# A mixture-of-experts stage rebuilt from four masked experts for every token to lists of one expert each

## What is computed

```python
x = hidden_states.reshape(-1, H)                     # 4096 tokens, H = 128, already normalised
expert_idx = jnp.argmax(x @ W_router, axis=-1)       # one of E = 4
h = jnp.einsum('th,ehi->tei', x, W1) + b1            # I = 512
h = jax.nn.gelu(h, approximate=False)
onehot = jax.nn.one_hot(expert_idx, E, dtype=x.dtype)
intermediate = jnp.einsum('te,tei->ti', onehot, h)
y = intermediate @ Wo + bo + x                       # Wo is one matrix for all experts
y = _layer_norm(y, ln_gamma, ln_beta)                # eps 1e-12
...
x = x + _layernorm(_L0_ffn_ref(_layernorm(x, axis=-1), ...), axis=-1)
```

## Time and profile before

| | us |
|---|---|
| median of 3 runs | 560.15 (558.89 to 562.59) |
| the profiled execution | 559.23 |
| its span, first to last instruction | 557.4 |
| TensorE busy | 506.9 |
| VectorE busy | 424.0 |
| GpSimd busy | 338.8 |
| ScalarE busy | 298.3 |

### The profile page before, as it was taken

One profiled execution on the slowest core, in us unless ns is written; L12 is line 12 of the kernel. 1 busy time (PEld: TensorE's weight loads), 2 busy tenths in 40 slices (PEclk: granted clock), 3 DMA queues, 4 the chain that ended last, 5 costly groups with the idle time before them and its releaser, 6 DMA issues. The chain is left out here.

```text
span 557.4 us, 16662 instructions
## 1 busy us (share of the span) xinstructions
PE 506.9 (91%) x5277; PEld 312.7 (56%) x5280; DVE 424.0 (76%) x1954; ACT 298.3 (54%) x820; POOL 338.8 (61%) x799
## 2 busy tenths in 40 slices
PE   8878679999999999999999998869999999999991
PEld 3434324556556665555555665535677677577671
DVE  5986696988888888998899887645647777675655
ACT  2665305888888888888888888713212211211110
POOL 4799202688888888688888889960122343333241
PEclk9999855999999999999999999989999999999997
DMA  4466450332112332123331100000000000000001
GB/s 128 137 214 176 150 98 2 101 92 69 49 27 59 81 63 64 38 41 63 62 64 40 27 4 4 4 1 1 0 1 1 20 19 0 19 20 0 20 19 38
DMA packets 49058, 28.09 MB, mean 50 GB/s; under 512 B 6808, under 2 KB 48056, under 8 KB 48976
## 3 DMA queue, kind: packets, MB, share of 16 engines
q1 hardware_dynamic: 47648, 26.73, 19.0%
q10 hardware_dynamic: 1328, 0.36, 0.3%
HBM read 17.90 MB, written 8.91 MB: 48 GB/s over the span
## 5 line engine op out<-in xcount | busy, mean ns | idle before, releaser
L1096 DVE CUSTOM_DVE_ANT_0 added<-psS,maskq 128x256 bf16<-128x256 f32 x512 | 200.5, 414 | 34.8 <-PE psS L937 21.9
L1316 ACT ACTIVATE probs<-psST 128x512 f32<-128x512 f32 x240 | 143.2, 597 | 43.2 <-PE psST L973 41.7
L973 PE MATMUL psST<-qst,kst 50*128 50x128 bf16 x992 | 101.0, 222 | 0.0
L937 PE MATMUL psS<-kst,qst 48*128 48x256 bf16 x448 | 91.5, 286 | 2.4 <-DVE rowmax L1096 1.3
L994 PE MATMUL psPV<-probs,vst 128*10 128x128 f32 x1984 | 79.9, 277 | 11.9 <-POOL probs L1231 8.1
L1760 ACT ACTIVATE hT<-fpsH 128x512 f32<-128x512 f32 x32 | 19.1, 597 | 121.7 <-PE fpsH L1504 121.7
L1228 POOL TENSOR_SCALAR_AFFINE_SELECT probs<-probs 128x256 f32<-128x256 f32 x150 | 61.7, 412 | 4.3 <-ACT probs L1316 4.1
L1231 POOL TENSOR_SCALAR_AFFINE_SELECT probs<-probs 128x256 f32<-128x256 f32 x150 | 61.2, 408 | 0.0
L937 PEld LDWEIGHTS psS<-kst,qst 48*128 48x128 bf16 x448 | 25.2, 95 | 62.6 <-issue 36.3
L994 PEld LDWEIGHTS psPV<-probs,vst 128*10 128x10 f32 x1984 | 43.9, 91 | 27.1 <-issue 16.6
L973 PEld LDWEIGHTS psST<-qst,kst 50*128 50x128 bf16 x992 | 55.8, 95 | 0.0
(11 more groups left out here) (198 smaller groups left out, 1092.5 us busy)
## 6 DMA issues: line engine op xcount, KB each, us to landing
q_parts<-early SPq DMA_DIRECT2D x8, 384.0 KB, 2.6
k_parts<-early SPq DMA_DIRECT2D x8, 384.0 KB, 2.7
qst<-q_parts SPq DMA_DIRECT2D x32, 96.0 KB
kst<-k_parts SPq DMA_DIRECT2D x32, 96.0 KB
X<-in_L_attn_x_dram SPq DMA_DIRECT2D x8, 256.0 KB, 3.3
qst<-q_parts SPq DMA_DIRECT2D x32, 64.0 KB
kst<-k_parts SPq DMA_DIRECT2D x32, 64.0 KB
out_dram<-res SPq DMA_DIRECT2D x8, 256.0 KB, 2.3
```

What stands on the lines that cost most here:

```text
L937: last = nc.tensor.matmul(bank[:, a], q, kst[rows, slot, ring(n - 1, 2)], start=True, stop=True)
L973: last = nc.tensor.matmul(bank[:, a, side * P:(side + 1) * P], kst[rows, slot, ring(n - 1 + side)], qst[rows, slot, ring(n)], start=not ma ...
L1096: taken = nc.vector.tensor_tensor_reduce(added[:, 2 * (g % 2) + a], psS[g % 2][:, a], mask, 1.0, NEG * 4, ALU.add, ALU.max, rowmax[:, n.mo ...
L1316: nc.scalar.activation(probs[:, g ^ 1], psST[g % 2][:].rearrange("p a c -> p (a c)"), ACT.Exp, scale=SCALE).then_inc(s_exp.sem, 1)
```

## The change

`attend` writes the residual to columns 128 to 255 of a new tile `rows` (257 floats for each token; column 256 holds the token's number, by an `iota` in `project`). In steps 3 to 21 of `attend`, ScalarE's queue issues one DMA a step that fills a block of 512 rows of the new DRAM tensor `by_expert` with blank rows (19 blocks of 526 KB). `project` gains 33 small `memset`s and one of 128 x 256 on VectorE. The bias is loaded by partition (`b1T`, four DMAs of 4-byte pieces), and nine VectorE operations that prepared the bias in three parts, and one on ScalarE, go; one small one (`tri`) comes.

`ffn` has two parts now:

1. Routing, chunk by chunk (8): turn, copy, logits, one-hot row with a sign (`choose`, 6 VectorE operations), the token's rank in its expert's list by small matmuls with a triangle of ones (`ranks`), its place (`places`, 5 VectorE operations), and on GpSimd four indirect DMAs of 128 rows of 1028 bytes to these places in `by_expert` (`move`). Experts 0 and 1 share a region and grow from its two ends, as do 2 and 3. Then `map_slots`, some 22 dependent VectorE operations on 11 to 44 columns, works out which expert and which block each of 11 slots has.
2. Slots (11, of 512 rows of one expert; 8 chunks and at most 3 partly filled blocks more): SyncE reads the numbers into a register, copies that expert's weights within SBUF (2 DMAs of 256 KB) and loads the block. TensorE turns it, and makes only the 12 matmuls of the one expert (before: 48 and 4 for the bias). The bias goes into ScalarE's GELU. Spread, mask and multiply are gone. Layer norms as before, split otherwise over the engines: VectorE the first and its statistics, ScalarE the second (`normed`). GpSimd writes the results by four indirect DMAs of 128 rows of 512 bytes, to the rows that column 256 names; blank rows lie out of bounds and are dropped.

```diff
+SLOT = CH
+NS = NCH + E - 1
+PAIR_ROWS = T + SLOT
+PAIR_SLOTS = PAIR_ROWS // SLOT
+SPARE = 2 * PAIR_SLOTS
+ROW = 2 * D + 1
...
+            nc.vector.memset(held.blank[:, 0:2 * D], 0.0)
+            nc.vector.memset(held.blank[:, 2 * D:ROW], 1.0)
...
+                    if g == 7 and 3 <= s.k < 3 + SPARE + 1:
+                        block = s.k - 3
+                        act.dma_start(by_expert[block * SLOT:(block + 1) * SLOT].rearrange("(t p) w -> p t w", p=P),
+                                      held.blank[:].unsqueeze(1).broadcast_to([P, CT, ROW])).then_inc(s_blank, 16)
...
+            def load_weights(i):
+                r = i % W_RING
+                e = sp.value_load(expert[0:1, i:i + 1], min_val=0, max_val=E - 1)
+                sp.wait_ge(s_h.sem, s_h.after(nth_slot(i - W_RING)))
+                for k, parts in enumerate((w1hi, w1lo)):
+                    sp.dma_start(w1[:, r, k].bitcast(F32),
+                                 parts[:, bass.ds(e, 1)].rearrange("k o i -> k (o i)").bitcast(F32)).then_inc(s_w1[r], 16)
+            def load_tile(i):
+                r = i % TILE_RING
+                a = sp.value_load(slot[0:1, i:i + 1], min_val=0, max_val=SPARE)
+                if i >= TILE_RING:
+                    n = i - TILE_RING
+                    sp.wait_ge(s_store[n % 2], 16 * CT * (n // 2 + 1))
+                sp.dma_start(tile[:, r], by_expert.rearrange("(n t p) w -> p n t w", p=P, t=CT)[:, bass.ds(a, 1)]
+                             .rearrange("p o t w -> p (o t) w")).then_inc(s_tile[r], 16)
+            sp.wait_ge(s_map, MAPPED)
+            for i in range(W_RING):
+                load_weights(i)
+            sp.wait_ge(s_moved, 16 * NB)
+            for i in range(W_RING):
+                load_tile(i)
+            for i in range(W_RING, NS):
+                load_tile(i)
+                load_weights(i)
...
+            def ranks(c):
+                pe.wait_ge(s_oh.sem, s_oh.after(c))
...
+                nc.tensor.matmul(psP[:, 0:CT * E], held.tri[:], flat, start=True, stop=False)
+                for t in range(1, CT):
+                    nc.tensor.matmul(psP[:, t * E:CT * E], filler[:, 0:P], flat[:, 0:(CT - t) * E], start=False,
+                                     stop=(t == CT - 1))
+                for t in range(CT):
+                    last = nc.tensor.matmul(psP[:, CT * E:(CT + 1) * E], filler[:, 0:P], signed[:, t],
+                                            start=(t == 0), stop=(t == CT - 1))
+                last.then_inc(s_rank.sem, 1)
+            turned(chunk(0))
+            logits(chunk(0))
+            for c in range(NCH):
+                keep_warm(nc, psY[1][:], filler, 4)
+                ranks(chunk(c))
+                if c + 1 < NCH:
+                    turned(chunk(c + 1))
+                    logits(chunk(c + 1))
+            keep_warm(nc, psY[1][:], filler, 24)
...
+            def hidden(n, j):
+                u, r = n.mod(2), n.k % W_RING
+                pe.wait_ge(s_gelu.sem, s_gelu.after(n, j + 1 - 2))
+                if j == 0:
+                    pe.wait_ge(s_w1[r], 32 * (n.k // W_RING + 1))
+                    pe.wait_ge(s_lo.sem, s_lo.after(n))
+                cols = slice(j * P, (j + 1) * P)
+                for k, (w, x) in enumerate(((0, xhi), (1, xhi), (0, xlo))):
+                    last = nc.tensor.matmul(psH[j % 2][:], w1[:, r, w, cols], x[:, u], start=(k == 0), stop=(k == 2))
+                last.then_inc(s_h.sem, 1)
...
+            for i in range(-1, NS + 1):
+                n = nth_slot(i)
+                if (n + 1).live:
+                    transposed(n + 1)
                 if n.live:
+                    hidden(n, 0)
+                    hidden(n, 1)
+                if (n - 1).live:
+                    outputs(n - 1)
                 if n.live:
+                    hidden(n, 2)
+                    hidden(n, 3)
...
+            def choose(c):
+                lg = psR[:, 0:CT * E].rearrange("p (t e) -> p t e", e=E)
+                dve.wait_ge(s_logit.sem, s_logit.after(c))
+                nc.vector.tensor_reduce(lmx[:], lg, AX.X, ALU.max).then_inc(s_oh.sem, 1)
+                dve.wait_ge(s_oh.sem, s_oh.after(c, 1))
+                nc.vector.tensor_tensor(iseq[:], lg, lmx[:].unsqueeze(2).broadcast_to([P, CT, E]),
+                                        ALU.is_equal).then_inc(s_oh.sem, 1)
+                dve.wait_ge(s_oh.sem, s_oh.after(c, 2))
+                nc.vector.tensor_tensor(rank[:], iseq[:], prio[:].unsqueeze(1).broadcast_to([P, CT, E]),
+                                        ALU.mult).then_inc(s_oh.sem, 1)
+                dve.wait_ge(s_oh.sem, s_oh.after(c, 3))
+                nc.vector.tensor_reduce(rmx[:], rank[:], AX.X, ALU.max).then_inc(s_oh.sem, 1)
+                dve.wait_ge(s_oh.sem, s_oh.after(c, 4))
+                nc.vector.tensor_tensor(onehot[:], rank[:], rmx[:].unsqueeze(2).broadcast_to([P, CT, E]),
+                                        ALU.is_equal).then_inc(s_oh.sem, 1)
+                dve.wait_ge(s_oh.sem, s_oh.after(c, 5))
+                nc.vector.tensor_tensor(signed[:], onehot[:], held.sign[:].unsqueeze(1).broadcast_to([P, CT, E]),
+                                        ALU.mult).then_inc(s_oh.sem, 1)
+            def places(c):
+                dve.wait_ge(s_rank.sem, s_rank.after(c))
+                nc.vector.tensor_tensor(place[:], psP[:, 0:CT * E].rearrange("p (t e) -> p t e", e=E),
+                                        following[:].unsqueeze(1).broadcast_to([P, CT, E]), ALU.add)\
+                  .then_inc(s_place.sem, 1)
+                dve.wait_ge(s_place.sem, s_place.after(c, 1))
+                nc.vector.tensor_tensor(following[:], following[:], psP[:, CT * E:(CT + 1) * E], ALU.add)\
+                  .then_inc(s_place.sem, 1)
+                nc.vector.tensor_tensor(own_place[:], place[:], onehot[:], ALU.mult).then_inc(s_place.sem, 1)
+                dve.wait_ge(s_place.sem, s_place.after(c, 3))
+                nc.vector.tensor_reduce(place_f[:], own_place[:], AX.X, ALU.add).then_inc(s_place.sem, 1)
+                dve.wait_ge(s_place.sem, s_place.after(c, 4))
+                nc.vector.tensor_copy(where[:, c.times(CT):c.times(CT, CT)], place_f[:]).then_inc(s_place.sem, 1)
+
...
+            norm.statistics(dve, chunk(2))
+            for i in range(NCH):
+                c = chunk(i)
+                choose(c)
+                if (c + 3).live:
+                    norm.statistics(dve, c + 3)
+                if (c + 2).live:
+                    norm.apply(dve, c + 2)
+                places(c)
...
+            def low(n):
+                dve.wait_ge(s_hi.sem, s_hi.after(n))
+                nc.vector.tensor_tensor(xlo[:, u], psT[u][:], xhi[:, u].bitcast(F32), ALU.subtract).then_inc(s_lo.sem, 1)
+            def scaled(n):
+                u = n.mod(2)
+                dve.wait_ge(s_rs2.sem, s_rs2.after(n))
                 for t in range(CT):
+                    last = nc.vector.scalar_tensor_tensor(out=y2[:, t], in0=y1[:, t], scalar=mv2[:, u, t, 0:1],
+                                                          in1=gamma[:], op0=ALU.subtract, op1=ALU.mult)
+                last.then_inc(s_y2.sem, 1)
+                dve.wait_ge(s_y2.sem, s_y2.after(n))
+                dve.wait_ge(s_y5.sem, s_y5.after(n - 2))
                 for t in range(CT):
+                    last = nc.vector.scalar_tensor_tensor(out=y4[:, u, t], in0=y2[:, t], scalar=rstd2[:, u, t:t + 1],
+                                                          in1=beta[:], op0=ALU.mult, op1=ALU.add)
+                last.then_inc(s_y4.sem, 1)
+                dve.wait_ge(s_y4.sem, s_y4.after(n))
+                dve.wait_ge(s_rs3.sem, s_rs3.after(n - 2))
+                statistics(s_st3, n, 1, lambda t: y4[:, u, t], mv3)
...
+            def result(n):
+                u = n.mod(2)
+                dve.wait_ge(s_y5.sem, s_y5.after(n))
+                if n.k >= 2:
+                    dve.wait_ge(s_store[u], 16 * CT * (n.k // 2))
+                nc.vector.tensor_tensor(res[:, u], y5[:, u], tile[:, n.k % TILE_RING, :, D:2 * D], ALU.add)\
+                  .then_inc(s_res.sem, 1)
+            def summed(n):
+                u = n.mod(2)
+                dve.wait_ge(s_Y.sem, s_Y.after(n))
+                dve.wait_ge(s_XF.sem, s_XF.after(n))
+                nc.vector.tensor_tensor(y1[:], psY[u][:].rearrange("p (t d) -> p t d", t=CT), XF[:, u], ALU.add)\
+                  .then_inc(s_y.sem, 1)
+                dve.wait_ge(s_y.sem, s_y.after(n))
+                dve.wait_ge(s_rs2.sem, s_rs2.after(n - 2))
+                statistics(s_st2, n, 0, lambda t: y1[:, t], mv2)
+            for i in range(-1, NS + 4):
+                n = nth_slot(i)
+                if (n + 1).live:
+                    low(n + 1)
+                if (n - 2).live:
+                    scaled(n - 2)
+                if (n - 3).live:
+                    result(n - 3)
+                if (n - 1).live:
```

(75 more changed lines are left out.)

588 lines of the change are left out of this document (236 added, 352 removed).

## The result

The changed kernel takes 608.7 us (median of 4 runs, 607.22 to 609.31), the kernel before 561.3 beside it on the same chip: a ratio of 1.085, with a 95% interval of 1.080 to 1.089. The prediction was 587 us with a range of 545 to 640; the result lies above the band of 570 to 605 that the prediction held likeliest. The profiled execution had 609.26 us and a span of 607.5.

The account below looks back on a forecast made before the run. The prediction took TensorE to bound `ffn` before, and a loop through GpSimd's stores and VectorE after. Stage start 380.9, routing 52.2, tile load 4.5, slots 147.2 and 1.8 around the span gave 587 us, range 545 to 640.

Parts of the forecast that it names:

- rival (b): In the slots VectorE locks GpSimd out while it makes addresses: C = 14.6, total 631 us; chance 0.11.
- start of the stage: Work added ahead of `ffn` shifts its start from 375.9 to 380.9 us; removed bias operations in `attend` taken as 0.
- s: Time one indirect DMA's issue takes in GpSimd's queue: taken as 1.1 us, between bounds of 0.45 and 2.16.
- R: Routing's length, by GpSimd's 32 indirect DMAs or the map: max(17 + 32s, 46) us, 52 at s = 1.1.
- S: All slots with filling and draining: 98.8 + 44s, 147 us at s = 1.1.
- C: One slot's turn through GpSimd, VectorE and the four stores on GpSimd: 7.4 + 4s, 11.8 us at s = 1.1.
- Fill and drain: Ends of the slots: `scaled(1)` starts at 24 us; after nine turns come 8.1 + 8s us.
- Price 0: TensorE's clock drops after pauses in the slots cost nothing: some 2 us of 7.2, still under C.
- (a): Indirect DMA issue is cheap, s = 0.45: total 552 us, faster by 1.3%; chance 0.17.
- (c): Each indirect DMA issue takes 2.16 us: R = 86, S = 194, total 667 us; chance 0.06.
- (e): The slots' loop is as priced but s lies at 0.6 to 0.75: 558 to 565 us, no difference; chance 0.12.
- (d): Blank writes stall `attend` by 2.16 us a step: total 624 us; chance 0.04.

Follow-up runs that it names:

- 3: Changed kernel with twelve filler matmuls on TensorE ahead of each slot's first hidden group: 614.15 us, ratio 1.099 to the kernel before.
- 8: Changed kernel with half of the routing's indirect DMAs left out (two of four tiles of each chunk not moved): 603.2 us, ratio 1.079 to the kernel before.
- 5: Changed kernel with the first norm's root ahead of the stores, `XF` replaced by one-row bias matmuls on TensorE, `low` after `scaled`: 597.73 us, ratio 1.068.
- 10: Changed kernel with the first norm's root ahead of the stores and eight filler matmuls a slot on TensorE: 588.71 us, ratio 1.052 to the kernel before.
- 1: Changed kernel with the first norm's root put ahead of the four indirect stores in GpSimd's order: 577.02 us, ratio 1.034 to the kernel before.

## Why the prediction came out as it did

The sign and the mechanism were right, and the time lies in the range, 22 us over the forecast. That the miss isn't larger is in part luck: three terms were together 31 us too low, and the start of the stage, put 8 us too late, hid a quarter of that. The upper end of the range came from rival (b), not from the terms that ran over. Of the signs that the prediction gave, the turn came out at 13.8 us and not 11 to 12, and TensorE's busy share in the slots at 69% (85.17 of 124 us) and not 60%. Term by term (us):

| term | forecast | measured |
|---|---|---|
| start of the stage | 380.9 | 372.9 |
| routing to the last landing | 52.2 | 56.8 |
| tile load to the first transposes | 4.5 | 4.7 |
| slots, first transposes to the end | 147.2 | 173.2 |
| around the span | 1.8 | 1.8 |

**The bound of the kernel before.** Right. With TensorE's work gone, nothing on it sets the turns of the changed kernel (3).

**The issue's price s.** The term was mis-sized: 1.28 for 1.1. It is in the routing 32 times and in the slots 44. By the prediction's own formulas R = 17 + 32 x 1.28 = 58, and 56.8 were measured; S = 98.8 + 44 x 1.28 = 155, 8 of the missing 26 us. s was taken between the 1.02 and 1.28 of the earlier trace rows. The instruction's own 0.97 lies below both, and the 0.30 us between two DMAs, which no row of before could show, make the pitch the upper of the two.

**The turn.** C = 7.4 + 4s gives 12.5 with the right s, and 13.8 were measured. 0.9 is `XF` against the affine group (4 shows it by leaving `XF` out), 0.35 is `ve` beside `res`, and the first store's longer issue is 0.1; these come to 1.35 for the missing 1.3. The prediction took `with_bias` as lying beside the loop. Its own time does, but not what it does to VectorE. It looked for a lock the other way round, in rival (b), and cited the earlier trace rows against one, though it said itself that those VectorE operations have one input. The affine steps have two, and that was not followed up.

**Fill and drain.** The third `scaled` starts 40.1 us after the first transposes, where 24 + 12.5 = 36.5 follow from the prediction; the fill runs at a clock of 0.61 (430 to 446 us), where the first slot's twelve matmuls take 5.5 us (437.37 to 442.89) for 2.80. From the last `scaled` (584.05) to the end it is 23.4 us for 18.3, of which 0.4 is the indirect DMA beside `res`. The last indirect DMA begins to issue at 600.05, and the span ends 7.5 us later; the plain DMA that ends the kernel before starts at 554.70 in a span of 557.4, 2.7 us. All other kernels with indirect stores end 7.4 to 7.5 after the last issue, but for 8 with 6.2. A landing inside the slots takes 2.2, so what fills the other 5 us isn't seen in the records and stays open. With the turn (8 from the third `scaled` to the eleventh, 13.7 us on average for 12.5) these are 3.6 + 5.1 + 9.5, and with the 7.9 of s they come to 26.1, the 26.0 us by which the slots took longer. (The prediction's own terms give 98.7 + 44s, not 98.8.)

**Ahead of the stage.** Wrong in sign, 8 us too late. The 19 issues of ScalarE, the memsets and the blank writes together cost some 2.1 us, not 5, and the bias operations that go gave 5.1 where they were put at 0, with an end of -2 that was too narrow. These nine operations stand on VectorE in `attend`, which they hold for 5.4 us, and each has a wait for the one before it; the prediction had no row of theirs.

**Routing.** GpSimd's queue ends it, as forecast, and its first move comes at 381.27, 8.4 us into the stage, as forecast too. The map's slot numbers are there 48.5 us in (421.34), not 46. A chunk takes 5.5 us on average and not 4.9: with the logits at half the clock (1.87 us for the 1.03 of the earlier trace rows) it is 5.4, and where VectorE's `apply` waits for a root behind four moves in GpSimd's queue it is 6.4 and 6.5. The map is still 8.3 us ahead of the last landing. What is close is what the prediction gave no price, the weights that it wrote are copied before: the six copies hold SyncE's queue from 422.50 to 428.12, and experiment 8 shows that they leave only 3.5 us to gain.

**TensorE's clock.** Price 0 was right for the turns (3), although the granted clock was 0.80 over the slots. It was wrong for the fill, where TensorE is on the path (3) and runs in part at half the clock; how much of the 3.6 us that is was not measured. The row that the prediction read gives 1.3 us for a drop (4 us at 0.67), not 2. The Trainium skill's rule (TensorE: Matmul & The Clock Gate, HAM oscillation), that bursts parted by waits each start at half the clock, agrees with the trace, 1.12 against 0.60 us. In the turns it costs nothing, because the wait for the tile is hidden, and it does cost in 5 and 10, where the wait is in the loop.

**The rivals.** (a), (c) and (e) fall with s = 1.28. (b) had a real mechanism at the wrong size: 1 has 1.10 to 1.16 us beside short two-input operations of VectorE, the drain has one DMA of 1.37 beside a long one, and in the changed kernel's turns the stores meet none; so the 2.8 us a turn did not come. (d): the blank writes are part of the 2.1 us. What no rival had was the tile ring as the bound behind GpSimd.

## What to carry to other kernels

Price an indirect DMA by the instruction and not by its bytes, and put what other engines wait for ahead of a run of them in GpSimd's queue: here the order of two calls was worth 5%. When an operation is called hidden, ask what it does to its neighbours (a GpSimd operation of 1.17 us under a VectorE operation with two inputs cost VectorE 0.9 a turn), and look one loop further, for rings whose release depends on the end of the pipeline: the loop through the tile ring took over as soon as the first was broken. Dividing the work by its kind has its price in front and at the ends: here 61 us of routing that nothing covers, and some 63 us of filling and draining.

## What the runs showed of the hardware

- An indirect DMA of 128 rows of 512 bytes holds GpSimd's queue for 0.97 us, one of 64 rows for 0.91, and in both 0.30 pass to the next. The first of a group of four takes 1.07 to 1.08, and those of the routing, with rows of 1028 bytes, take the same 0.97 to 0.98 behind the first of each group.
- Beside VectorE operations of 0.34 us with two SBUF inputs it took up to 1.16 us, and beside one of 0.69 us (`res`) 1.37 to 1.40. A tensor operation of GpSimd and such a VectorE operation hold each other up by nearly their whole length: 2.06 us for a group of 1.14 (changed kernel), 2.09 for an operation of 0.66 (1), and 0.55 for GpSimd's `ve` of 0.20 to 0.23.
- A bias matmul over one row took 0.41 us to the start of the next (500.19 to 500.60 in 5), the four over 128 rows behind it 1.09 (to 501.69), so 0.27 each. Fewer rows to sum over made it no cheaper.
- A program that ends in indirect DMAs of GpSimd ended 7.4 us after the last began to issue, one that ends in a plain DMA 2.7.
